# A graph attention and expert kernel: the node rows are prepared left half first, then right half, with eight groups of edge rows gathered in the second half

## What is computed

```python
def gnn(xn, src, dst, w):                      # xn = layernorm(x)
    x_l = (xn @ W_l + b_l).reshape(n, H, C)    # left rows, taken by src
    x_r = (xn @ W_r + b_r).reshape(n, H, C)    # right rows, taken by dst
    x_j = x_l[src]
    g = leaky_relu(x_r[dst] + x_j, 0.2)
    alpha = einsum('ehc,hc->eh', g, att) + log(w)[:, None]
    ex = exp(alpha - segment_max(alpha, dst)[dst])
    alpha = ex / (segment_sum(ex, dst)[dst] + 1e-16)
    return segment_sum(x_j * alpha[..., None], dst).reshape(n, H*C) + bias
x = x + gnn(layernorm(x), src, dst, edge_weight)
x = x + ffn(layernorm(x))   # top 2 of 8 experts, 256 -> 512 -> 256, exact gelu
```

## Time and profile before

| | |
|---|---|
| Three runs | 1834.54, 1837.83, 1844.31 us; median 1837.83 |
| The profiled execution: from its first to its last instruction | 1834.0 us |
| `prepare`, to the first instructions of `edges` | 0 to 151.1 us |
| `edges`: first to last gather issued | 152.9 to 1260.5 us |
| `edges`: first to last take-over of a sum by ScalarE | 164.8 to 1276.1 us |
| `experts` | from about 1435 us to the end |
| TensorE busy, whole program | 1704.0 us (93%), mean granted clock 0.962 |

### The profile page before, as it was taken

The page is one execution under the profiler, slowest core; times in us unless marked ns, Lnnn a source line. Parts: engine busy times, 40 slices in busy tenths (PEclk is TensorE's granted clock), DMA queues, the critical chain, the costliest instruction groups (busy, mean ns, idle before and its releaser), DMA issues. The chain is left out here.

```text
span 1834.0 us, 36250 instructions
## 1 busy us (share of the span) xinstructions
PE 1704.0 (93%) x9433; PEld 1449.1 (79%) x9434; DVE 1417.0 (77%) x2670; ACT 1250.3 (68%) x3163; POOL 1299.3 (71%) x1358
## 2 busy tenths in 40 slices
PE   6895789999999999999999999998797899999998
PEld 4674578887787888788888888876596799999998
DVE  6774689999999999999999999999868433333333
ACT  3463589999898999999999999987770133233222
POOL 4866777777777777777777777776435677776775
PEclk9997899999999999999999999999857999999999
DMA  6887777877877888777878888774674344444444
GB/s 224 225 267 248 220 235 239 240 242 238 238 243 236 240 241 240 238 244 243 235 245 239 241 241 243 240 236 130 202 244 166 73 78 70 72 71 69 70 73 52
DMA packets 214752, 359.18 MB, mean 196 GB/s; under 512 B 44062, under 2 KB 103880, under 8 KB 214457
## 3 DMA queue, kind: packets, MB, share of 16 engines
q1 hardware_dynamic: 150392, 208.33, 34.9%
q0 software_dynamic: 63072, 147.92, 33.3%
q10 hardware_dynamic: 1120, 1.05, 0.2%
HBM read 302.77 MB, written 54.40 MB: 195 GB/s over the span
## 5 line engine op out<-in xcount | busy, mean ns | idle before, releaser
L829 POOL DMA_INDIRECT rows<-left_rows,idx x880 | 841.1, 956 | 269.3 <-issue 263.9
L1191 PE MATMUL p_row<-rights,hotT 128*128 128x256 f32 x1760 | 504.0, 368 | 55.4 <-issue 26.0
L1193 PE MATMUL p_row<-rows,ident 128*128 128x256 f32 x1760 | 529.8, 383 | 0.0
L1254 PE MATMUL p_gain<-W,hots 128*128 128x264 f32 x1760 | 470.4, 391 | 8.7 <-DVE acc L1029 6.3
L1191 PEld LDWEIGHTS p_row<-rights,hotT 128*128 128x128 f32 x1760 | 322.0, 192 | 131.1 <-issue 82.1
L1254 PEld LDWEIGHTS p_gain<-W,hots 128*128 128x128 f32 x1760 | 324.0, 190 | 78.9 <-issue 24.6
L1081 ACT ACTIVATE L<-p_row 128x512 f32<-128x512 f32 x440 | 259.2, 589 | 127.0 <-PE p_row L1193 125.3
L1708 ACT ACTIVATE e_hT<-e_ph,b_column 128x128 f32<-128x128 f32 x420 | 119.7, 368 | 326.0 <-PE e_ph L1733 326.0
L1000 DVE TENSOR_TENSOR W<-rows,p_weights 128x1024 f32<-128x1024 f32 x220 | 266.9, 1213 | 43.9 <-PE p_gain L1254 41.4
L1151 ACT ACTIVATE far<-iota_row,dl 128x128 f32<-128x128 f32 x880 | 299.2, 391 | 0.0
L909 DVE TENSOR_TENSOR L<-L,p_weights 128x1024 f32<-128x1024 f32 x220 | 266.1, 1210 | 27.0 <-ACT L L1081 27.0
(11 more groups left out here) (254 smaller groups left out, 1880.7 us busy)
## 6 DMA issues: line engine op xcount, KB each, us to landing
rights<-right_rows SPq DMA_DIRECT2D x440, 256.0 KB
locals<-item_locals SPq DMA_DIRECT2D x110, 256.0 KB, 3.7
rows<-left_rows,idx POOLq DMA_INDIRECT x880
right_rows<-p_parts SPq DMA_DIRECT2D x49, 256.0 KB
w<-in_L_ffn_W SPq DMA_DIRECT2D x16, 512.0 KB, 6.4
left_rows<-p_y SPq DMA_DIRECT2D x49, 132.0 KB
kept_rows<-X SPq DMA_DIRECT2D x7, 896.0 KB, 4.4
X<-kept_rows SPq DMA_DIRECT2D x7, 896.0 KB, 4.9
```

Source lines behind the costliest of these rows:

```text
L829: nc.gpsimd.indirect_dma_start(out=rows[:, g.slot(RINGS), n, :], out_offset=None, in_=d["left"][:, :], in_offset=bass.IndirectOffsetOnAxis ...
L1191: nc.tensor.matmul(to, hotT[:, g.slot(2), i, :], rights[:, g.slot(2), n, part * D:(part + 1) * D], start=(part == 0), stop=False)
L1193: last = nc.tensor.matmul(to, s["ident"][:, :], rows[:, g.slot(RINGS), i, 0:D], start=False, stop=True)
L1254: last = nc.tensor.matmul(p_gain[:, n, 0:D + H], hots[:, g.slot(2), i, :], W[:, g.slot(2), i, :, :].rearrange("p h c -> p (h c)"), start=( ...
```

## The change

In `prepare` the 49 tiles are gone through twice: first all left rows, then all right rows.

- ScalarE copies the turned rows into `X` itself, where they stay for the second pass (`xT` is gone).
- The biases become a third product for each tile and side: `bias_ones` (33 x 128) by `bias_parts` (33 x 256), float32r. Row 0 holds the high part and row 32 the low part of b_l + bias (left) or b_r - bias (right). Seven instructions on VectorE make them, ahead of its first statistics.
- Left rows are copied to `y` by ScalarE (even tiles) and VectorE (odd tiles). Both parts of the right rows are made by VectorE, straight from PSUM. `py` is a ring of four banks.
- GpSimd has no work on rows left: neither the additions to `X` nor the low parts. `kept_rows` is neither written nor read; the rows of `x` are read again from the input, the last batch with three DMAs.
- After its 21 fetches GpSimd waits until all left tiles have landed, then gathers groups 0 to 7 in the second pass, group g once the right product ceil((g+1) x 1056 / 256) is done, because the ring lies over the turned rows.
- `edges` starts its gathers at group 8 and reads the source list in place: the copies on VectorE (L893) and their waits are gone.
- The item steps stand at other turns, the log weights and marks in the second pass. `x` is loaded in four pieces, not three.

The diff, cut to its core:

```diff
+EARLY_GROUPS = 8
+BIAS_ROWS = 33
+SRC_TURN, LOCAL_TURN, WEIGHT_TURN = 27, 37, 10
+ROOT_BEFORE, SCALE_BEFORE, STATS_BEFORE, MOMENTS_BEFORE = 5, 4, 7, 6
+MARKS_AFTER = (20, 26, 30)
-PIECES = ((0, BY), (BY, 4 * BY), (4 * BY, 7 * BY))
+PIECES = ((0, BY), (BY, 2 * BY), (2 * BY, 4 * BY), (4 * BY, 7 * BY))
@@ GpSimd
-                for t in range(-2, NODE_TILES):
-                        nc.gpsimd.tensor_tensor(X[:, t + 2, :], X[:, t + 2, :], out_bias[:, :], ALU.add)
...
-                        nc.gpsimd.tensor_tensor(parts[:, t % 4, 1, :], right[:, t % 4, :], parts[:, t % 4, 0, :], ALU.subtract
...
+                pool.wait_ge(turned_copied, QI)
+                for k in range(4):
+                    pool.wait_ge(left_stored[k], 16 * len(range(k, NODE_TILES, 4)))
+                for g in range(EARLY_GROUPS):
+                    pool.wait_ge(right_projected, min(NODE_TILES, -(-(g + 1) * G * DL // D)))
+                    wait(pool, gathered[g % RING], g // RING * (16 * G))
+                    for n in range(G):
+                        gather_item(nc, d, s, g, n)
@@ SP
+                for t in range(NODE_TILES):
+                    sp.wait_ge(*left_of(t))
+                    sp.dma_start(d["left"][t * P:(t + 1) * P, :], y[:, t % 4, :]).then_inc(left_stored[t % 4], 16)
...
+                for t in range(NODE_TILES):
+                    sp.wait_ge(low_done, t + 1)
+                    sp.dma_start(d["right"][t * P:(t + 1) * P, :], parts[:, t % 4, :, :].rearrange("p a f -> p (a f)")
+                                 ).then_inc(right_stored[t % 4], 16)
@@ TensorE
+                def multiply(t, slot, side, wide, done):
+                    for h in range(KD):
+                        nc.tensor.matmul(py[:, slot, 0:wide], X[:, t, h * P:(h + 1) * P],
+                                         W[:, h, side, 0:wide], start=(h == 0), stop=False)
+                    nc.tensor.matmul(py[:, slot, 0:D], bias_ones[:, :], bias_parts[:, side, :], start=False, stop=True
+                                     ).then_inc(done, 1)
+                def project_right(t):
+                    if t < 4:
+                        pe.wait_ge(*left_of(NODE_TILES + t - 4))
+                    else:
+                        pe.wait_ge(low_done, t - 3)
+                    multiply(t, right_slot(t), 1, D, right_projected)
@@ VectorE
+                def take_high(t):
+                    v.wait_ge(right_projected, t + 1)
+                    wait(v, right_stored[t % 4], 16 * (t // 4))
+                    nc.vector.tensor_scalar(parts[:, t % 4, 0, :].bitcast(I32), py[:, right_slot(t), 0:D].bitcast(I32),
+                                            LOW_BITS, LOW_BITS, ALU.logical_shift_right, ALU.logical_shift_left)
+                def take_low(t):
+                    v.wait_ge(high_done, t + 1)
+                    nc.vector.tensor_tensor(parts[:, t % 4, 1, :], py[:, right_slot(t), 0:D], parts[:, t % 4, 0, :], ALU.subtract)
+                v.wait_ge(biases_in, 48)
@@ edges
-                             (listed, g.turn(TURN) + 1))
+                    if g.n >= EARLY_GROUPS:
+                        wait(pool, weighed, g.n - (RINGS - 1))
+                        wait(pool, gathered[g.slot(RING)], g.turn(RING) * (16 * G))
+                        for n in range(G):
+                            gather_item(nc, d, s, g.n, n)
-                     (-2, bind), (-1, sweep_back), (-2, carry_over), (TURN - 1, list_ahead), (0, empty),
+                     (-2, bind), (-1, sweep_back), (-2, carry_over), (0, empty),
```

More of the change, by code:

```diff
@@ L151, in build @@
             left=dram("left_rows", (NODE_TILES * P, DL)),
-            right=dram("right_rows", (NT * P, 2 * D)), kept=dram("kept_rows", (NODE_TILES * P, D)),
+            right=dram("right_rows", (NT * P, 2 * D)),
             normed=dram("normed_rows", (NODE_TILES * P, D)),
@@ L167, in build @@
             pass
+        s["gathered"] = [nc.alloc_semaphore(f"g_gathered{i}") for i in range(RING)]
         s["rows"] = keep("rows", [P, RINGS, G, DL])
@@ L268, in blocks_in, with left_of, right_slot @@
             return min(P, EB - c * P)
[L270 to L274, removed]
+        def left_of(t):
+            return (left_by_vector, (t + 1) // 2) if t % 2 else (left_by_scalar, t // 2 + 1)
+        def right_slot(t):
+            return (NODE_TILES + t) % 4
         with nc.Block(no_gpsimd_drain=True) as block:
@@ L313, in _ @@
                 nc.gpsimd.memset(pad_k[:, :], -2.0).then_inc(pads_set, 1)
[L314 to L318, removed]
@@ new lines, in _ @@
+                pool.wait_ge(biases_in, 48)
+                nc.gpsimd.memset(no_edges[:, :, C:C + 1], 0.0)
+                nc.gpsimd.tensor_scalar(no_edges[:, :, 0:C], bias_rows[:, 2, :].rearrange("p (h c) -> p h c", c=C), 1e-16, None, ALU.mult)
+                pool.wait_ge(items_done, 1)
+                for rows, table, landed in ((rows_s, "src", src_in), (rows_d, "dst", dst_in), (rows_w, "weight", weight_in)):
+                    for q in range(QI):
+                        nc.gpsimd.indirect_dma_start(
+                            out=rows[:, q, :], out_offset=None, in_=d[table][:, :],
+                            in_offset=bass.IndirectOffsetOnAxis(ap=t_idx[:, q:q + 1], axis=0),
+                        ).then_inc(landed, 16)
@@ L534, in _ @@
+                act.wait_ge(floored, 1)
+                nc.scalar.activation(rows_w[:, :, :], rows_w[:, :, :], ACT.Ln).then_inc(logged, 1)
+                for q in range(QI):
+                    copy_back(2 * QI + q, s["logw"])
             @block.vector
@@ L693, in _, with gather_item @@
                         last.then_inc(breaks_done, 1)
+def gather_item(nc, d, s, g, n):
+    i = g * G + n
+    nc.gpsimd.indirect_dma_start(
+        out=s["rows"][:, g % RINGS, n, :], out_offset=None, in_=d["left"][:, :],
+        in_offset=bass.IndirectOffsetOnAxis(ap=s["srcs"][:, i:i + 1], axis=0),
+    ).then_inc(s["gathered"][g % RING], 16)
 def node_tiles(eng, regs, s, g):
@@ L732, in edges @@
     matched, cleared = sem("g_matched"), sem("g_cleared")
-    listed = sem("g_listed")
-    gathered = [sem(f"g_gathered{i}") for i in range(RING)]
+    gathered = s["gathered"]
     rights_in = [sem(f"g_rights_in{i}") for i in range(2)]
@@ L887, in _ @@
                 v.wait_ge(cleared, 2)
-                def list_sources(g):
-                    if g.c % TURN == 0:
-                        for r in range(RING):
-                            wait(v, gathered[r], (g.turn(RING) - 2) * (16 * G))
-                        nc.vector.tensor_copy(idx[:, parity(g), :], s["srcs"][:, bass.ds(g.n * G, CHUNK)]).then_inc(listed, 1)
-                def list_ahead(g):
-                    if not isinstance(g.n, int) or g.n > 0:
-                        list_sources(g)
                 def empty(g):
```

357 lines of the change are left out of this document (166 added, 191 removed).

## The result

The changed kernel takes 1852.14 us (median of 5 runs, 1848.08 to 1857.26) beside 1837.83 for the kernel before (of five runs too, 1834.54 to 1844.31): ratio 1.0072, 95% interval 1.0050 to 1.0094. It is slower, by 14 us (0.7%). The forecast was 1826.5 with a range of 1806 to 1846. The profiled execution took 1857.26 us, 5 above the median, its span is 1855.3.

What follows compares the result with a forecast made beforehand. GpSimd's gather issue was taken to bound `edges`, TensorE with stalls `prepare`. +16 us at the entry and -27 in `edges` gave -11 on the 1834.0 span, 1823; 3.8 more for the median: 1826.5, range 1806 to 1846.

Steps and rivals of the forecast that it cites:

- Bias product: In `prepare`, the added float32r product per tile and side costs 0.13 us, no dearer with fewer rows, no cheaper than 0.
- Start: Start of `prepare`: bias parts ahead of the first statistics on VectorE delay them 7 us, to 16.3; first turn at 22.7.
- Left half: First pass of `prepare`: 49 left tiles 63 us, small products and the like 9.6, stalls 5; ends at about 101 us.
- Right half: Second pass of `prepare`: transfers bound it at 60 us (53 to 72), TensorE needs 46, VectorE 53; ends at 161 us.
- The profile's sign that was named: In the right half, VectorE would wait for stores, with the DMA share near 1.
- `edges`, -27: In `edges`, groups 0 to 7 gathered early: last gather 1084 us after entry instead of 1110.8, 27 us less (18 to 38).
- The stop before group 16: In `edges`, GpSimd stops some 19 us before group 16 for the first weighting, its only gap.
- the sign that the text named: In `edges`, many GpSimd gaps for weightings after group 16 would mean the forecast is wrong and TensorE bounds.
- Cheap preparation: Rival in `prepare`: no left stalls, transfers not in the way, biases in early; `edges` entered 2 us later, 1813 us; chance 0.22.
- The head start worth little: Rival in `edges`: TensorE's own pace is 5.0 us a group, the early start gives about 17 us; 1837 us; chance 0.15.
- Gathers held by VectorE: Rival in the right half: VectorE's parts slow the 32 early gathers to 72 us, entry at 182; 1842 us; chance 0.05.
- Four buffers: Rival in the right half: stores landing from 5.5 us on set the tiles; at 6.5 us, 95 us and 1862; chance 0.08.

Runs made afterwards that it cites:

- rows128_again: Repeat run of the changed kernel with the bias product filled to 128 rows instead of 33, still float32r: 1829.36 us, ratio 0.9946 to the kernel before.
- no_bias: The changed kernel without the two bias products, so the biases are left out of the rows: 1824.95 us, ratio 0.9935 to the kernel before.
- early0: The changed kernel with no group gathered in the right half (0 early groups instead of 8): 1873.32 us, ratio 1.0200 to the kernel before.
- rows128: First run of the changed kernel with 128 rows in the bias product instead of 33: 2298.27 us, ratio 0.9881 to the kernel before at 2320.68.

## Why the prediction was wrong, step by step

The time is wrong by one term of the sum. Entry of `edges` and last gather in each profile:

| kernel | start: first transpose | left half | right half | entry T | last gather |
|---|---|---|---|---|---|
| forecast | 22.7 | 78 | 60 | 167 | T + 1084 |
| before | 15.50 | | | 151.1 | T + 1110.8 |
| changed | 21.46 | 95.5 | 68.4 | 189.3 | T + 1085.2 |
| rows128_again | 21.63 | 81.8 | 61.4 | 168.5 | T + 1084.3 |
| no_bias | 21.77 | 77.2 | 61.3 | 163.8 | T + 1085.9 |

Here the left half runs from the first transpose to the start of the last copy of `y` (the experiments count from the first copy, some 4 us later), the right half from the start of the first to the end of the last step on `parts`.

- *Bias product: the step that failed.* I priced a product of float32r at 0.13 us from pairs in `edges` and wrote "With fewer rows of depth it won't be dearer than this". All products of the earlier trace rows have 128 rows. With 128 rows the product measured 0.12, so the size taken from the rows was right; with 33 it is 0.51, since its load and the next each start 0.31 us after the product ahead, not with it. 98 of them at 0.39 too much are 38 us of TensorE, 21 us of which reached the entry (189.3 against 168.5): in the right half the transfers are the next limit at 61 us, only 7 below, and the left half was 13.7 us longer, not 19; part of the product's time there may have fallen into stalls that are there anyway. The entry was 22.3 us later than forecast; 1826.5 + 22.3 = 1848.8, and 1852.14 was measured. The text named over 0.2 us for this product as what would make it wrong; it was bounded by 0 and 0.13 in the range, and no rival had it.
- *Start.* +7 forecast, +6.0 measured. Right; the statistics began at 15.08, not 16.3.
- *Left half.* 63 + 9.6 + 5 = 78 us; 81.8 in rows128_again, so right within 4 us once the product costs what was taken. From the last parts to the entry it was 2.6 us, not 5.5, which takes most of that back.
- *Right half.* "The transfers bound this half, just: I take 60 us": wrong for the changed kernel (TensorE, 1.37 us a tile), right for rows128_again (61.4) and no_bias (61.3, DMA share 0.96 at 304 GB/s between 105 and 160 us). The profile's sign that was named, waits of VectorE for stores, was there with 9.2 us but behind TensorE's.
- *`edges`, -27.* Right: -25.6 against the kernel before, and -24.8 against early0. The stop before group 16 was 13.9 us, not 19, as the gathers of groups 8 to 15 went on to T + 45 (T + 41 forecast). It was not GpSimd's only wait: 46 more for weightings followed until 1275 us, 16.3 us in all, where the kernel before had 0.6 us in two. This is the sign that the text named for being wrong here (TensorE bounds). It cost little: each such wait takes the place of a gap of 0.3 us that stands ahead of a gather anyway, 14 us for the 46, so they cost 2 us. TensorE is nearly level with GpSimd, but doesn't bound.
- *Rivals.* Cheap preparation: out, it took 22 us more than the forecast, not 14 less. The head start worth little: out (early0 costs 21 us). Gathers held by VectorE: GpSimd was busy 32.26 us with 32 of them between 120 and 185 us, 1.01 us each; out. Four buffers: a store landed after 3.6 us in the median, where the rival needed 5.5, and 9.2 us of waits for stores were hardly a cost. Slower than before it was all the same, by a mechanism that none of them had.

"Its price shows nowhere" was not so either: the trace of the kernel before has products with few rows among products with 128, in `edges`. L1206 loads 16 rows, 84 times, mostly between `gain` (L1254) and the next sum, and its load stands off in the same way. The timeline of TensorE's weight loads in the kernel before:

```profile
602.39 0.85 PEld L1254 LDWEIGHTS p_gain<-W,hots 128*128 128x128 f32 x4
603.58 0.09 PEld L1206 LDWEIGHTS p_back<-marks_by_block,to_blocks 16*128 16x128 bf16 x1 [0.34 <-issue]
603.79 0.30 PEld L1191 LDWEIGHTS p_row<-rights,hotT 128*128 128x128 f32 x2
```

That load starts 0.31 us after the product ahead of it (603.27), and so do the loads with 8 rows on L1242. A row with fewer rows of depth was there to price the product from, and it would have spoken against 0.13 us.

## What to carry to other kernels

A price taken from the nearest row holds for the shape of that row: before a small product is costed at "not dearer than a big one", look in the trace of the kernel before for a product of the same number of rows, and whether its load and the next run beside products. Where products with fewer rows stand among products with 128, filling the rows with zeros can be cheaper than leaving them out: here 0.12 us instead of 0.51. And a head start need only be as long as the ring behind it can use: five groups did what eight did, within the noise. A clock column says nothing of a stretch in which the trace has no clock record; the length of a known weight load does.

## What the runs showed of the hardware that was not expected

- A float32r product with 33 rows between products with 128 costs 0.51 us, with 128 rows 0.12 us; two with 33 rows in a row share the gaps. Loads of 8 and 16 rows in `edges` also start 0.31 us after the product ahead. Whether 32 or 64 rows do the same was not tried, and nor was filling L1206 up to 128 rows.
- With a float32 product of one row at every tile TensorE stayed at 1.2 GHz through all of `prepare` (weight loads of 0.33 us instead of 0.19, first clock record at 379.8 us), though it was busy 342 of the 343 us from 22 to 365; why is open. With 33 rows in float32 it was granted 2.4 GHz from 24.5 us, and the granted clock fell to 0.50 in one stretch of the profiled run, with TensorE busy throughout.
- The same kernel of before took 1838 to 1840 us on four occasions and 2320.68 on another; there the DMA engines moved 168 GB/s in rows128 between 600 and 800 us, not 240. The three kernels with 128 rows were faster than it both times, but not in the same order (0.9881, 0.9862, 0.9920; then 0.9946, 0.9929, 0.9922).
